# A decoder layer on one core: the first tile of each sequence attends to its own 128 keys alone

## The reference

```python
x = x + _L0_attn_ref(_layernorm(x, axis=-1), L0_attn_W_qkv, L0_attn_W_out, L0_attn_b_out)
...
q = q * cos + _rotate_half(q) * sin
k = k * cos + _rotate_half(k) * sin
mask = (j <= i) & (j >= i - WINDOW)        # i: query, j: key, WINDOW = 128
scores = jnp.einsum('bhid,bhjd->bhij', q, k) * scale
scores = jnp.where(mask, scores, jnp.finfo(scores.dtype).min)
attn = jax.nn.softmax(scores, axis=-1)
out = jnp.einsum('bhij,bhjd->bhid', attn, v)
```

## Time and profile before

| | before |
|---|---|
| median of 3 runs | 1598.3 us (1596.05 to 1601.76) |
| the profiled execution | 1598.66 us |
| its span, first to last instruction | 1596.9 us |
| TensorE busy, its weight loads | 1405.2 us (88%), 1037.1 us (65%) |
| VectorE, ScalarE, GpSimd busy | 1041.5, 973.5, 760.2 us |
| mean granted TensorE clock | 0.946 |

### The profile page before, as it was taken

How to read it: one execution, slowest core, us unless ns; L and a number is a source line. 1 busy time by engine, 2 the same in 40 slices (tenths; PEclk the granted TensorE clock), 3 DMA queues, 4 the chain that set the end, 5 groups by cost and what they waited for, 6 DMA issues and landing times. The chain is left out here.

```text
span 1596.9 us, 27909 instructions
## 1 busy us (share of the span) xinstructions
PE 1405.2 (88%) x9603; PEld 1037.1 (65%) x9603; DVE 1041.5 (65%) x1953; ACT 973.5 (61%) x1969; POOL 760.2 (48%) x492
## 2 busy tenths in 40 slices
PE   3999999999857588998999989749999999999990
PEld 2777777777645443444444433439999999999980
DVE  4677676777545524545555567548888888888870
ACT  3666666666522155765666677427777777777760
POOL 2444544544410034633624610026777777777862
PEclk9999999999988789999999999759999999999995
DMA  9000000000012393493492490448999999999977
GB/s 340 1 14 28 24 18 28 14 28 15 14 52 95 78 141 77 99 168 104 93 176 92 93 188 5 150 133 243 295 294 298 302 298 298 295 296 290 299 148 131
DMA packets 133107, 229.77 MB, mean 144 GB/s; under 512 B 17865, under 2 KB 51145, under 8 KB 132496
## 3 DMA queue, kind: packets, MB, share of 16 engines
q1 hardware_dynamic: 101168, 151.30, 34.3%
q0 software_dynamic: 29248, 72.53, 20.3%
q10 hardware_dynamic: 2592, 4.65, 1.1%
HBM read 163.78 MB, written 71.83 MB: 148 GB/s over the span
## 5 line engine op out<-in xcount | busy, mean ns | idle before, releaser
L1030 ACT ACTIVATE shared<-xa_ring 128x1024 f32<-128x1024 f32 x256 | 246.5, 1026 | 74.4 <-PE xa_ring L1451 74.2
L992 POOL TENSOR_TENSOR shared<-shared,xa_half 128x32 f32<-128x32 f32 x24 | 130.3, 5428 | 233.5 <-DVE shared L1159 233.5
L1625 POOL DMA_INDIRECT ex_xg<-xn,token x128 | 173.9, 1359 | 80.4 <-issue 61.5
L354 ACT ACTIVATE sa_prob<-sa_sc_ps,sa_nmax 128x256 f32<-128x256 f32 x256 | 117.8, 472 | 93.5 <-DVE sa_nmax L446 93.5
L300 POOL TENSOR_TENSOR sa_prob<-sa_prob,sa_rinv 128x1024 f32<-128x1024 f32 x64 | 121.1, 1893 | 95.6 <-DVE sa_rinv L459 95.6
L95 PE MATMUL ex_ba<-ex_xh,ex_wh 128*128 128x256 f32 x512 | 150.6, 294 | 3.7 <-DVE ex_xl L1739 3.7
L96 PE MATMUL ex_ba<-ex_xl,ex_wh 128*128 128x256 f32 x512 | 145.6, 284 | 0.0
L97 PE MATMUL ex_ba<-ex_xh,ex_wl 128*128 128x256 f32 x512 | 145.6, 284 | 0.0
L1726 DVE TENSOR_TENSOR ex_wl<-shared,ex_wh 128x1024 fp32r<-128x1024 f32 (+1 forms) x128 | 116.9, 955 | 36.2 <-ACT ex_wh L1669 36.1
L1463 PE MATMUL xa_out<-shared 128*17 128x512 f32 x1024 | 138.2, 612 | 0.4 <-ACT shared L1030 0.4
L1451 PE MATMUL xa_ring<-xa_qT,xa_kT 48*128 48x512 f32 x512 | 102.2, 465 | 14.3 <-ACT shared L1030 11.3
(11 more groups left out here) (227 smaller groups left out, 4000.0 us busy)
## 6 DMA issues: line engine op xcount, KB each, us to landing
shared<-in_L_ffn_gate_proj_dram SPq DMA_DIRECT2D x64, 384.0 KB, 5.8
shared<-in_L_ffn_up_proj_dram SPq DMA_DIRECT2D x64, 384.0 KB, 7.8
turned<-stage SPq DMA_DIRECT2D x64, 256.0 KB, 2.8
shared<-in_L_ffn_down_proj_dram SPq DMA_DIRECT2D x64, 256.0 KB, 5.4
xa_kT<-turned SPq DMA_DIRECT2D x96, 128.0 KB, 8.1
xa_qT<-turned SPq DMA_DIRECT2D x96, 128.0 KB, 10.6
shared<-in_L_ffn_down_proj_dram SPq DMA_DIRECT2D x64, 128.0 KB, 6.8
sa_x<-in_x_dram SPq DMA_DIRECT2D x16, 256.0 KB, 2.6
```

The lines of the kernel that those rows point to most:

```text
L354: act.activation(prob[:, h, :], sc_ps[p][:, i, :], ACT.Exp, bias=nmax[:, h:h + 1], accum_out=rsum[:, h:h + 1]).then_inc(s_ex[p], 1)
L992: pool.tensor_tensor(power[:, i], ms[:, i], half[:], ALU.pow).then_inc(s_pw, 1)
L1030: act.activation(prob[:, w % 2, 2 * i:2 * i + 2, :], ring[i][:], ACT.Exp, scale=D2 ** -0.5).then_inc(s_ex[i], 1)
L1625: pool.indirect_dma_start(out=xg[:, e % RING, j, :], out_offset=None, in_=xn3, in_offset=bass.IndirectOffsetOnAxis(token[:, at:at + 1], 0))\
```

## The change

A tile now knows which blocks it has: `sides()` is one block for t = 0 and two otherwise, and `width()` is 128 or 256 columns. For a first tile the mask product, the QK products, the maximum, the exponentials and the scaling take 128 columns of each head instead of 256; the bank layout stays. `turn_prob` makes four transposes instead of eight, `values` uses one block, and VectorE's `take_prob` returns at once, without a wait and without a count. Because of that the counts of the second bank's copies (`s_pt[1]`, `s_pe[1]`) no longer equal the number of groups; `with_past(k)` gives how many of the first k groups belong to tiles with t > 0, and the waits use it. The two clears of `kT` and `v` at the start are gone, and GpSimd waits for three clears there instead of five.

```diff
@@ -160,10 +160,8 @@
             def _(pool):
                 pool.memset(half[:], -0.5).then_inc(s_z, 1)
                 pool.memset(eps[:], LN_EPS).then_inc(s_z, 1)
-                pool.memset(kT[:].bitcast(F32), 0.0).then_inc(s_z, 1)
-                pool.memset(v[:], 0.0).then_inc(s_z, 1)
                 pool.memset(zero[:], 0.0).then_inc(s_z, 1)
-                pool.wait_ge(s_z, 5)
+                pool.wait_ge(s_z, 3)
             def parts(c):
                 if c < C:
@@ -233,9 +231,20 @@
             def ahead(self, i):
                 return Tile(self.b, self.t + i)
+            def sides(self):
+
+                return range(1 if self.t == 0 else 2)
+
+            def width(self):
+                return len(self.sides()) * P
+
             def exists(self):
                 return 0 <= self.n < NT
+
+        def with_past(k):
+
+            return sum(i // 4 % T > 0 for i in range(k))
         def tiles(engine, tile):
@@ -297,8 +306,8 @@
                     if g in (1, 2) and at.ahead(1).exists():
                         rotate(at.ahead(1), g - 1)
                     pool.wait_ge(s_ri, START + at.k(g) + 1)
-                    pool.tensor_tensor(prob[:, 4 * g:4 * g + 4, :], prob[:, 4 * g:4 * g + 4, :],
-                                       rinv[:, 4 * g:4 * g + 4].unsqueeze(2).to_broadcast([P, 4, 2 * P]),
+                    part = prob[:, 4 * g:4 * g + 4, 0:at.width()]
+                    pool.tensor_tensor(part, part, rinv[:, 4 * g:4 * g + 4].unsqueeze(2).to_broadcast([P, 4, at.width()]),
                                        ALU.mult).then_inc(s_pn, 1)
                     if g == 3 and at.ahead(-1).exists():
                         add_bias(at.ahead(-1))
@@ -351,7 +360,7 @@
                         act.wait_ge(s_mx, START + 2 * at.k(g) + p + 1)
                         for i in range(2):
                             h = 4 * g + 2 * p + i
-                            act.activation(prob[:, h, :], sc_ps[p][:, i, :], ACT.Exp, bias=nmax[:, h:h + 1],
+                            act.activation(prob[:, h, 0:at.width()], sc_ps[p][:, i, 0:at.width()], ACT.Exp, bias=nmax[:, h:h + 1],
                                            accum_out=rsum[:, h:h + 1]).then_inc(s_ex[p], 1)
                     if g > 0:
                         take_prob(at, g - 1)
@@ -426,7 +435,9 @@
                 dve.tensor_copy(kT[:, 4 * g:4 * g + 4, at.t % 2, :], tn_ps[1][0:3 * D1]).then_inc(s_ke, 1)
             def take_prob(at, g):
-                dve.wait_ge(s_pt[1], START + at.k(g) + 1)
+                if at.t == 0:
+                    return
+                dve.wait_ge(s_pt[1], START + with_past(at.k(g)) + 1)
                 dve.tensor_copy(pT[:, 1], tn_ps[1][:]).then_inc(s_pe[1], 1)
             def low_out(at):
@@ -443,7 +454,7 @@
                     for p in range(2):
                         dve.wait_ge(s_sc[p], START + at.k(g) + 1)
                         h = 4 * g + 2 * p
-                        dve.tensor_reduce(nmax[:, h:h + 2], sc_ps[p][:], AX.X, ALU.max, negate=True).then_inc(s_mx, 1)
+                        dve.tensor_reduce(nmax[:, h:h + 2], sc_ps[p][:, :, 0:at.width()], AX.X, ALU.max, negate=True).then_inc(s_mx, 1)
                     if g in (1, 2) and nxt.exists():
                         rotate(nxt, g - 1)
                     if g == 1 and last.exists():
@@ -540,8 +551,9 @@
                         pe.wait_ge(s_lo, START + 2 * n + i + 1)
                     if k > 0:
                         pe.wait_ge((s_qe, s_ke)[i], START + k)
-                        if k > 1:
-                            pe.wait_ge(s_pe[i], START + k - 1)
+                        copied = k - 1 if i == 0 else with_past(k - 1)
+                        if copied > 0:
+                            pe.wait_ge(s_pe[i], START + copied)
                     for j in range(4):
                         done = pe.transpose(tn_ps[i][0:3 * D1, j, :], stack[:, at.t % 2, i, 4 * g + j, :].bitcast(F32),
                                             ident[:])
@@ -551,7 +563,7 @@
                 k = at.k(g)
                 pe.wait_ge(s_pn, START + k + 1)
                 heads_read = min(k + 2, 4 * NT)
-                for i in range(2):
+                for i in at.sides():
                     pe.wait_ge((s_qe, s_ke)[i], START + heads_read)
                     for j in range(4):
                         done = pe.transpose(tn_ps[i][:, j, :], prob[:, 4 * g + j, i * P:(i + 1) * P], ident[:])
@@ -564,12 +576,12 @@
                     if at.ahead(-1).exists():
                         pe.wait_ge(s_oh, START + at.n)
                         pe.wait_ge(s_ol, START + at.n)
-                for i in range(2):
-                    pe.wait_ge(s_pe[i], START + k + 1)
+                for i in at.sides():
+                    pe.wait_ge(s_pe[i], START + (k if i == 0 else with_past(k)) + 1)
                     keys = at.t if i == at.t % 2 else (at.t - 1) % T
                     for j in range(4):
                         done = pe.matmul(out_ps[32 * j:32 * j + 32, g, :], v[:, keys, 4 * g + j, :], pT[:, i, j, :],
-                                         start=(i == 0), stop=(i == 1))
+                                         start=(i == 0), stop=(i == at.sides()[-1]))
                 done.then_inc(s_pv, 1)
             def scores(at, g):
@@ -580,11 +592,12 @@
                 for p in range(2):
                     if k > 0:
                         pe.wait_ge(s_ex[p], START + 2 * k)
-                    pe.matmul(sc_ps[p][:], identb[:], mask[:, kind].unsqueeze(1).to_broadcast([P, 2, 2 * P]), start=True,
-                              stop=False)
+                    pe.matmul(sc_ps[p][:, :, 0:at.width()], identb[:],
+                              mask[:, kind, 0:at.width()].unsqueeze(1).to_broadcast([P, 2, at.width()]), start=True, stop=False)
                     for i in range(2):
                         h = 4 * g + 2 * p + i
-                        done = pe.matmul(sc_ps[p][:, i, :], qT[:, h, :], kT[:, h].rearrange("p a b -> p (a b)"),
+                        done = pe.matmul(sc_ps[p][:, i, 0:at.width()], qT[:, h, :],
+                                         kT[:, h].rearrange("p a b -> p (a b)")[:, 0:at.width()],
                                          start=False, stop=(i == 1))
                     done.then_inc(s_sc[p], 1)
```

## The result

The changed kernel took 1587.05 us (median of 8 runs, 1581.93 to 1592.61) against 1598.55 us (8 runs, 1595.31 to 1610.29): ratio 0.9913, 95% interval 0.9889 to 0.9936, about 11.5 us. The forecast was 1586. The profiled span is 1585.6 us (1596.9 before), the mean granted clock 0.949 (0.946 before).

The account below looks back on a forecast made before the run. The prediction took self-attention's time as the sum of TensorE's steps, with ScalarE's chain almost level. Scores 4.3, transposes 5.3 and values 3.2 made 12.8 us off 1598.7, so 1586 us, range 1582 to 1594.5.

Parts of the forecast that it names:

- Scores: First tiles' mask and QK products: a unit saves 0.13 us, a group 0.27, sixteen groups 4.3 us.
- in proportion: Rival: a QK product at half width costs half, 0.06 us; 16.0 us gained in all, 1582.7; chance 0.15.
- price of 0.11: Assumed step of a 128-column QK product, 0.11 us, taken from transposes and router; saves 0.01 each.
- f32 price: Rival: a narrow QK product costs two passes, 0.22 us; only 5.7 us gained in all, 1593.0; chance 0.28.
- Transposes: Four of eight probability transposes go, 0.44 us a group; twelve groups count, 5.3 us.
- Values: Values product of first tiles' groups: sixteen records become eight, 0.20 us a group, 3.2 us.
- all 16 count: Claim that the values saving counts in every group, including those falling into the next tile's group 0; 3.2 us.
- ScalarE's chain in first tiles: Chain shrinks to 3.18 us, TensorE last at 3.24; rival: chain stays 3.80, total 1591.5, chance 0.07.
- cover of 0.02: Margin in us by which TensorE reached the next heads' transposes after ScalarE's chain: 3.95 against 3.93.
- The clock: Granted clock stays at 1.00 in self-attention; rival: a fall in each of 16 groups, 1613.9 us, chance 0.05.
- GpSimd, clears, waits: Shorter scaling, two clears gone, no wait added: all beside TensorE's time, worth nothing.
- lost later: Rival: the next stage's waits grow by as much as self-attention gains; total about 1598, chance 0.05.

Follow-up runs that it names:

- qk_split: Changed kernel with every QK product of two-block tiles issued as two products of 128 columns; 1601.33 us (one run).
- transposes_twice: Changed kernel with a first tile's own block transposed a second time into the second bank, which VectorE copies; 1590.26 us, ratio 0.9946 to the kernel before.
- values_twice: Changed kernel with a first tile's values product issued twice; 1585.49 us, ratio 0.9918 to the kernel before.
- early_take: Changed kernel with ScalarE copying the last group's transposed probabilities after two of four exponentials, in all tiles; 1581.86 us, ratio 0.9870 to the kernel before.
- width_wide: Changed kernel with a first tile's scores, maximum, exponentials and scaling back at 256 columns; 1598.05 us, ratio 0.9985 to the kernel before.
- copy_first: Kernel before, with VectorE's copy of the second bank moved ahead of its other work in groups 1 to 3; 1597.82 us, ratio 0.9992.
- scores_wide: Changed kernel with only a first tile's mask and QK products back at 256 columns a head; 1592.3 us, ratio 0.9955 to the kernel before.
- later_sequences: Changed kernel with narrow first tiles only in sequences 2 to 4, the first worked as before, both clears back; 1586.68 us, ratio 0.9926 to the kernel before.
- after_shift1: Changed kernel with one more clear on VectorE before the first tile's row statistics, moving self-attention's start; 1584.83 us (one run).

## Why the prediction was right, point by point

The mechanism was right: TensorE's steps set the stage, and leaving them out shortened it one for one, as long as ScalarE's chain shrank with them. That the total came within 1.1 us of the forecast is in part luck: the sum's terms were off in both directions, and what was not foreseen nearly cancelled.

- *Scores*, forecast 4.3 us: 5.2 measured (16 groups of 2 x 0.163). The step that failed is the saving of a QK product, put at 0.01 each. Starts within a unit show where the 0.163 lies; the second QK product and the next mask product, first before, in the unit that begins at 143.03, then with the unit's begin in the changed kernel:

```profile
143.37 0.28 PE L587 MATMUL sa_sc_ps<-sa_kT,sa_qT 96*128 96x256 f32 x1
143.49 0.39 PE L583 MATMUL sa_sc_ps<-sa_mask,sa_identb 128*128 128x512 bf16 x1
```

```profile
142.43 0.28 PE L595 MATMUL sa_sc_ps<-sa_mask,sa_identb 128*128 128x256 bf16 x1
...
142.61 0.27 PE L599 MATMUL sa_sc_ps<-sa_kT,sa_qT 96*128 96x128 f32 x1
142.73 0.28 PE L595 MATMUL sa_sc_ps<-sa_mask,sa_identb 128*128 128x256 bf16 x1
```

From the mask product to the second QK product it is 0.34 us before, 0.18 in the changed kernel, and 0.29 in qk_split, where the mask product is wide and the QK product narrow (0.345, 0.182 and 0.286 in the mean of all units at full clock). So the mask product saves 0.10, the QK product right behind it 0.06, as in proportion, and the second almost nothing (0.12 in both kernels), as forecast. The price of 0.11 thus holds behind another QK product, and fails behind the mask product; the f32 price (0.22) fell. The Trainium skill (TensorE: Matmul & The Clock Gate, section Back-to-back issue gap) calls the formula that the prediction quoted, 56 ns at 128 columns, the gap of a product on its own, and gives about 81 ns for a stream of weight loads and products, which I passed over. Where one narrow QK product follows another, the runs have 0.11 us, above both figures.
- *Transposes*, forecast 12 x 0.44 = 5.3: transposes_twice gives 0.43 to 0.44 each, 5.2. Right, with the four of group 3 lost in the next tile's group 0, as forecast.
- *Values*, forecast 16 x 0.20 = 3.2: 12 x 0.22 = 2.6. The step that failed is "all 16 count". In the next tile's group 0 I held ScalarE's chain at 3.93; it is 168.38 - 164.25 = 4.13, because the maximum began 0.66 us after the first score before and now begins 0.85 after. VectorE's two instructions ahead of it start 0.34 us before the first score, where they started 0.56 before it: TensorE's group 3 became shorter, and VectorE's work in it did not. values_twice and early_take show that this group's time belongs to the chain.
- *ScalarE's chain in first tiles*: exponentials 0.366 us (forecast 0.38), maximum 0.414 (0.43), no stop in groups 1 to 3 of a first tile in sequences 2 to 4. (In the first sequence TensorE stands 1.44 us for ScalarE in group 3, 1.54 before.) The rival fell; width_wide shows what a chain at full width would have made of it: 24.47 us a tile, with wide scores.
- *Not foreseen, a gain*: that TensorE never rests in a tile was wrong by 0.14 us in groups 1 and 2. It waited some 0.05 for ScalarE ahead of the heads' transposes (in group 0 too; early_take takes it away there), where the prediction had a cover of 0.02, and 0.09 within them for VectorE's copy, which I had called "beside TensorE: nothing" (copy_first). No line shows either as a stop. In first tiles both go: 8 x 0.09 + 12 x 0.05 = 1.3 us. For the second wait, narrow maxima are enough (transposes_twice has the copy and no stand), and so is leaving out the copy (width_wide has wide maxima and no stand). With this a first tile's 25.41 - 21.82 = 3.59 us is placed: scores 1.3, transposes 1.3, values 0.65, the two waits 0.2 and 0.15.
- *Tiles*: first tile 22.4 forecast, 21.82 measured; the tile after 25.2 forecast, 25.39; the others 25.4, as measured. The two together save 3.62 us a sequence, forecast 3.2.
- *The clock*: the forecast "stays at 1.00" failed. Two falls in the first sequence cost some 2.8 us, an estimate: scores_wide, without them, took 20.99 + 25.19 = 46.18 for its two tiles, less 1.27 for the scores 44.91; the changed kernel took 47.70. The rival had them in every first tile; those of sequences 2 to 4 ran at 1.00. And I had written that the clock fell once in this stage before, at 450.5. It fell twice; the kernel before has this stretch in its last tile as well:

```profile
427.00:430.40 3.40, 3.40 (x27) 2.35 (x26) 1.39 (x3) 1.14 (x3) 0.79 (x1) 0.53 0.00 0
```

- *GpSimd, clears, waits*: at nothing, as forecast. Scaling takes 1.04 us instead of 1.89, and the clears' absence left the first score at 43.90 (43.59 before).
- *After the stage*: it begins as much earlier as this one ends, 6.22 us after instead of 6.29. Cross-attention took 1.5 us more, so not all of the gain reached the total. Whether the change caused that is not shown: over all runs this stage, the same code, took between 595.8 and 609.8 us. The rival "lost later" is neither borne out nor excluded at that size.

The 13.0 us are thus: three later sequences 3 x 3.62 = 10.9; the first sequence's two tiles 0.9 (48.60 to 47.70, the falls taken off); the last tile and its projection 1.5, of which 0.9 lie behind the last group's start, where the projection no longer ran at half clock; the stage's start -0.3, at 43.90 instead of 43.59. Forecast 12.8.

**What stays open.** Why the clock falls where it does. The first of the two falls came in all runs with narrow scores in the first tile, but also in later_sequences, width_wide and copy_first, whose first group had its old work, and not in scores_wide. The second came in all runs whose first tile was the changed kernel's in full (five runs, qk_split among them), and in none where that tile had a part of its work back or early_take's order. A stop of TensorE stands ahead of it (1.44 us in the changed kernel), but values_twice has 1.43 us there and the kernel before 1.54, and neither a fall. Open, too, is why cross-attention, the same code in all runs, took between 595.8 and 609.8 us; no order by the moment at which it begins is to be seen (604.2 at 447.8 us, 601.0 at 448.2 in after_shift1, 609.8 at 439.5, 602.7 at 460.8).

## What to carry to other kernels

Where two chains run level, as TensorE's and ScalarE's here, work left out of one pays only if the other shrinks in the same place; look for the group into which deferred work falls, since there the cut side arrives early and waits. Price a narrower operation by bounds, and for each place that it has in the stream: here the same halving saved 0.06 us behind one product and almost nothing behind another. Look for stands inside a run of equal instructions: a row of eight that took 1.15 us where others took 1.05 held a wait. A saving of under one per cent is moved by a stage later on by about as much as its own terms were uncertain, so compare stage ends and not only totals.

## What the runs showed of the hardware that was not expected

A product of the rounded 4-byte type that follows another one stepped by 0.11 us at 128 columns (qk_split) and 0.12 at 256: splitting it cost time, and narrowing it saved almost none. Behind the bf16 mask product the same narrowing saved 0.06. ScalarE's exponential took 0.366 us at 128 columns and 0.473 at 256, so halving saved 0.107; another line's, at 64 columns, took 0.336. VectorE's maximum fell from 0.686 to 0.414 us at half width, GpSimd's scaling from 1.89 to 1.04.
